# Layer 1's four wide chunks as a split group, its subtraction on VectorE

## The chip, the cores and the metric

The kernel runs on one core of a Trainium2 chip. The metric is the time of one execution on the device, in microseconds (us), and the time shown is the median of several runs. A separate execution, recorded by the hardware profiler, gives the profile and the trace.

## The reference

A "compressed interaction network" of three layers over x0 of shape 512 x 32 x 64 (batch, field, depth). Each layer multiplies every row of its input h with every row of x0, mixes the products with a weight matrix, adds a bias and applies ReLU:

```
for i in range(3):
    Wk = Ws[i].reshape(128, H, 32)              # H = 32 in layer 1, 64 in layers 2 and 3
    xk = relu(einsum('bhd,bmd,ohm->bod', h, x0, Wk) + b[i])
    if i != 2:  outs.append(xk[:, :64]); h = xk[:, 64:]
    else:       outs.append(xk)
y = concatenate([o.sum(axis=-1) for o in outs], axis=1)     # 512 x 256
```

All arithmetic is in float32.

## The kernel before, in words

The 512 x 64 (batch, depth) pairs are 32768 columns, in 64 tiles of T = 512 columns. Products of rows h and m of one tile are laid out as chunks of 128 partitions: layer 1 needs 5 chunks (the symmetric pairs are folded by adding two weight arrangements), layers 2 and 3 need 16 each, taken as four groups (q = 0 to 3) of G = 4 chunks. A chunk is one matmul of a 128x128 weight with a 128x512 product.

A float32 matmul takes two passes of TensorE. A group can be *split* instead: ScalarE rounds the product ZS to a type that TensorE multiplies in one pass (`high`, ZH), GpSimd or VectorE subtracts to get the rest (`low`, ZL = ZS - ZH), and the weights are split in the same way at the start. Three sets of four fast matmuls (WL x ZH, WH x ZH, WH x ZL) then stand in for four float32 ones. Groups 0, 1 and 3 of layers 2 and 3 are split; group 2 is *plain* (float32, through the wide buffer ZW), and so is all of layer 1 (four chunks through ZW, the fifth through the narrow buffer ZN).

All orders are written out by hand, with one instruction stream for each engine and semaphores between them. Iteration i works on layer 1 of tile i, layer 2 of tile i-1 and layer 3 of tile i-2.

- VectorE (L252 to L278) makes the products: layer 1 and ZN (L199), four of layer 2, the sum of layers 1 and 2 (L237), four of layer 3, with one subtraction (L228, that of layer 2's group 3) after layer 3's first product, then the sum of layer 3 (L242). Layer 1's product reads XDP, which is the copy in PSUM of XD; the others read HP, the copy in PSUM of H. All read X from SBUF.
- ScalarE (L340 to L363) does the rounding (L313), the copies of XD (L300) and of H (L306), and the ReLUs (L324, L329, L332). The copy of XD for tile i+1 stands between the rounding of layer 2's group 3 and that of layer 3's group 0.
- GpSimd (L280 to L292) does five subtractions a tile (L291).
- TensorE (L410 to L434): layer 1, layer 2, layer 3, in that order.
- SyncE (L160 to L172) issues all DMAs, on one queue, in this order in iteration i: XD of tile i+1 (four pieces of 64 KB, L139), X of tile i+1 (four pieces of 512 KB, L134), the spread of H of tile i after layer 1's ReLU, the spread of H of tile i-1 after layer 2's ReLU (L145, L148: five pieces inside SBUF).

ZS, ZH and ZL have three slots each. A product waits until the subtraction three groups back is done; a rounding and a subtraction wait until TensorE has finished the group three back. ZW has two slots, XD two, X four.

Of the kernel before, what the change touches and what calls it, by code (L numbers as in the profile page):

```python
# [6 lines left out]
HID, OUT = 64, 128  # L7
# [8 lines left out]
G = 4  # L16
Q = 4
PLAIN = 2
SPLIT = (0, 1, 3)
BY_DVE = ((1, 2),)  # L20
NS = len(SPLIT)
# [15 lines left out]
def wide_before(i, layer):  # L37

    n = sum(live(k - l) for k in range(i) for l in range(3))
    return n + sum(live(i - l) for l in range(layer))  # L40


def split_before(i, layer, k):

    n = NS * sum(live(s - l) for s in range(i) for l in (1, 2))
    return n + NS * sum(live(i - l) for l in range(1, layer)) + k


def lows_before(n, by_dve):

    order = [(layer, k) for i in range(TILES + 2) for layer in (1, 2) if live(i - layer) for k in range(NS)]
    return sum((u in BY_DVE) == by_dve for u in order[:n])


def cin_kernel(nc, xpad, w1, w1t, w2, w3, bias, ident_in, out):
# [4 lines left out]
    with ctx:  # L60
# [9 lines left out]
        W1 = sb("W1", [128, C1, OUT])  # L70
        WF = sb("WF", [128, 2, G, OUT])
# [6 lines left out]
        XD = sb("XD", [128, 2, T])  # L78
# [12 lines left out]
        WS = ZS[:, 0:2, 0:NS, :].rearrange("p w n (g o) -> p w n g o", g=G)  # L91
        OUTS = XD[:, :, :].rearrange("p a (b c) -> p (a b) c", b=2)
# [10 lines left out]
        w1_summed, w_high, w_low = sem("w1_summed"), sem("w_high"), sem("w_low")  # L103
        cleared = sem("cleared")
        x_loaded = [sem(f"x_loaded{n}") for n in range(XSLOTS)]
        xd_loaded = [sem(f"xd_loaded{n}") for n in range(2)]
# [14 lines left out]
        def wait_lows(engine, n):  # L121

            if lows_before(n, False):
                engine.wait_ge(low_by_pool, lows_before(n, False))
            if lows_before(n, True):
                engine.wait_ge(low_by_dve, lows_before(n, True))

        @block.sync
        def _(sp):
            def load_x(t):  # L130
                slot = t % XSLOTS
                for k in range(NB):
                    src = bass.AP(xpad.tensor, k * TOK + t * T, [[TOK, BLK], [NB * TOK, XC], [1, T]])
                    sp.dma_start(X[BLK * k:BLK * k + BLK, slot, :, :], src).then_inc(x_loaded[slot], 16)  # L134

            def load_xd(t):
                for k in range(NB):
                    src = bass.AP(xpad.tensor, t * T, [[TOK, BLK], [1, T]])
                    sp.dma_start(XD[BLK * k:BLK * k + BLK, t % 2, :], src).then_inc(xd_loaded[t % 2], 16)  # L139
# [12 lines left out]
            load_xd(0)  # L152
            load_x(0)
            sp.dma_start(bias_sb[:, :], bias).then_inc(small_loaded, 16)
            sp.dma_start(ident[:, :], ident_in).then_inc(small_loaded, 16)
            for w, wd in enumerate((w2, w3)):
                for n, q in enumerate(SPLIT):
                    sp.dma_start(WS[:, w, n, :, :], wd[:, G * q:G * q + G, :]).then_inc(ws_loaded[w], 16)  # L158
                sp.dma_start(WF[:, w, :, :], wd[:, G * PLAIN:G * PLAIN + G, :]).then_inc(wf_loaded[w], 16)
            for i in range(TILES + 2):  # L160
                t = i + 1
                if live(t):
                    if t >= 2:
                        sp.wait_ge(xd_copied, t - 1)
                    load_xd(t)
                    if t >= XSLOTS:
                        sp.wait_ge(prod_ready, split_before(t - XSLOTS + 2, 2, NS - 1) + 1)
                    load_x(t)
                if live(i):
                    spread_hidden(i, 0)  # L170
                if live(i - 1):
                    spread_hidden(i - 1, 1)  # L172
            for n in range(BLOCKS):
                sp.wait_ge(outs_ready, n + 1)
                sp.dma_start(out[128 * n:128 * n + 128, :], OUTS[:, n, :]).then_inc(stored, 16)
            sp.wait_ge(stored, 16 * BLOCKS)

        @block.vector
        def _(dve):
# [7 lines left out]
            dve.wait_ge(w1_summed, 4)  # L187

            def wide_slot(i, layer):
                n = wide_before(i, layer)  # L190
# [8 lines left out]
            def layer1(i):  # L199
                x = X[:, i % XSLOTS, :, :]  # L200
                to = wide_slot(i, 0)
                dve.wait_ge(xd_copied, i + 1)
                dve.wait_ge(x_loaded[i % XSLOTS], 16 * NB * (i // XSLOTS + 1))
                nc.vector.tensor_tensor(to, over(XDP[:, :], G), x[:, 0:G, :], ALU.mult).then_inc(wide_ready, 1)  # L204
                if i >= 1:
                    dve.wait_ge(narrow_used, i)
                nc.vector.tensor_tensor(ZN[:, :], XDP[:, :], x[:, G, :], ALU.mult).then_inc(narrow_ready, 1)

            def product(i, layer, q):
# [42 lines left out]
            for i in range(TILES + 3):  # L252
# [15 lines left out]
                if live(i - 1):  # L268
                    low(i, 1, 2)
# [11 lines left out]
        def _(pool):  # L281
            for i in range(TILES + 2):
                for layer in (1, 2):
                    for k in range(NS) if live(i - layer) else ():
                        if (layer, k) in BY_DVE:
                            continue
                        n = split_before(i, layer, k)
                        if n >= SSLOTS:
                            pool.wait_ge(split_used, n - SSLOTS + 1)
                        pool.wait_ge(high_ready, n + 1)  # L290
                        nc.gpsimd.tensor_tensor(ZL[:, n % SSLOTS, :, :], ZS[:, n % SSLOTS, :, :],  # L291
                                                ZH[:, n % SSLOTS, :, :], ALU.subtract).then_inc(low_by_pool, 1)  # L292

        @block.scalar
        def _(act):
            def copy_xd(t):
                act.wait_ge(xd_loaded[t % 2], 16 * NB * (t // 2 + 1))
                if t >= 1:
                    act.wait_ge(narrow_ready, t)
                nc.scalar.activation(XDP[:, :], XD[:, t % 2, :], ACT.Copy).then_inc(xd_copied, 1)  # L300

            def copy_hidden(t, layer):
                act.wait_ge(h_loaded[layer], 16 * (1 + NB) * (t + 1))
                if t >= 1:
# [29 lines left out]

            for w in range(2):
# [30 lines left out]
        def _(pe):  # L366
            def layer1(i):
                if i == 0:
                    pe.wait_ge(w1_summed, 4)
                else:  # L370
                    pe.wait_ge(relu_done[0], i)
                n = wide_before(i, 0)
                pe.wait_ge(wide_ready, n + 1)
# [6 lines left out]
            def plain(i, layer):  # L380
                n = wide_before(i, layer)
# [6 lines left out]
            def split(i, layer, q):  # L388
                k = SPLIT.index(q)
                n = split_before(i, layer, k)  # L390
# [7 lines left out]
                wait_lows(pe, n + 1)  # L398
# [11 lines left out]
            for i in range(TILES + 2):  # L410
                if live(i):
                    layer1(i)
                for layer in (1, 2):
# [7 lines left out]
                    for q in range(Q):  # L421
# [7 lines left out]
                        if q == PLAIN:  # L429
                            plain(i, layer)  # L430
# [38 lines left out]
```

## Time and profile before

| | |
|---|---|
| median of 3 runs | 1852.87 us (1852.87 to 1853.91) |
| profiled execution, its own time | 1851.87 us |
| its span | 1850.1 us |
| busy: TensorE, VectorE, GpSimd, ScalarE | 1799.3, 1552.2, 1468.3, 1095.6 us |
| DMA queue of SyncE | 204.68 MB, 52.5% of 16 engines' span |
| X, to landing, median of 256 pieces | 9.0 us |
| XD, to landing, median of 256 pieces | 2.0 us |

The busy time of an engine counts its instructions. A matmul's length in the trace is modelled and overlaps the next, so for TensorE the distance from one start to the next is what a matmul costs. VectorE's and ScalarE's instructions overlap their successors a little too. A bracket at the end of a timeline row gives the idle time of the engine before the instruction and what ended it.

### The profile page before, as it was taken

The numbers are of one execution on the slowest core, as the hardware profiler recorded it, in microseconds if no ns is written. First come the engines' busy times: TensorE is split into PE (matmuls) and PEld (weight loads), VectorE is DVE, ScalarE is ACT, GpSimd is POOL, SyncE is SP. The second block draws the span as 40 slices with busy tenths as digits, with TensorE's granted clock in tenths as the row PEclk, the third lists the DMA queues.
The fourth block names the chain that finished last, engine by engine and source line by source line (L and its number), as shares of the span: only waits on it lengthen the run. The fifth ranks groups of instructions, "written<-read, shape, count | busy, mean of one in ns | idle before, by whom it ended". The sixth has DMA issues, their size and how long they took to land.

```text
span 1850.1 us, 18063 instructions
## 1 busy us (share of the span) xinstructions
PE 1799.3 (97%) x6284; PEld 1184.3 (64%) x6284; DVE 1552.2 (84%) x853; ACT 1095.6 (59%) x899; POOL 1468.3 (79%) x324
## 2 busy tenths in 40 slices
PE   3899999999999999999999999999999999999997
PEld 1566666666666666666666666666666666666665
DVE  3998898898898888888888888888888888988974
ACT  2566656656656666566565665665666666566562
POOL 0788878878878778778778778778778788788786
PEclk9999999999999999999999999999999999999998
DMA  8565455465465564564564564564564554654610
GB/s 201 111 123 121 98 122 116 101 125 114 100 128 107 105 128 105 106 129 103 107 129 102 109 128 99 114 128 93 121 128 92 122 125 92 125 122 95 126 26 20
DMA packets 119513, 205.83 MB, mean 111 GB/s; under 512 B 18816, under 2 KB 19968, under 8 KB 119424
## 3 DMA queue, kind: packets, MB, share of 16 engines
q1 hardware_dynamic: 119424, 204.68, 52.5%
q8 instruction: 51, 0.84, 0.2%
q14 instruction: 38, 0.31, 0.1%
HBM read 153.75 MB, written 0.52 MB: 83 GB/s over the span
## 4 chain that ended last, share of the span: by engine, by line
PE 96%; POOL 1%; DMA 1%; SPq 1%; ACT 1%; DVE 0%; issue 0%; DVEq 0%; POOLq 0%; ACTq 0%
PE ACC L384 24%; PE ACC L400 19%; PE ACC L394 19%; PE ACC L397 19%; PE ACC L375 12%; PE ACC L378 3%; POOL ZL L291 1%; DMA ZS<-in_w 1%; ACT ZH L313 0%; DVE ZS L221 0%; SPq L158 0%; DVE ZW L204 0%; ACT HP L306 0%; DMA H<-H 0%; SPq L139 0%
## 5 line engine op out<-in xcount | busy, mean ns | idle before, releaser
L291 POOL TENSOR_TENSOR ZL<-ZS,ZH 128x2048 fp32r<-128x2048 f32 x320 | 1468.1, 4617 | 372.8 <-ACT ZH L313 372.8
L313 ACT ACTIVATE ZH<-ZS 128x2048 fp32r<-128x2048 f32 x384 | 734.2, 1912 | 536.7 <-PE ACC L400 415.0
L221 DVE TENSOR_TENSOR ZS<-HP,X 128x2048 f32<-128x2048 f32 x384 | 870.5, 2281 | 150.9 <-ACT HP L306 149.6
L394 PE MATMUL ACC<-ZH,WL 128*128 128x512 f32 x1536 | 497.5, 446 | 7.3 <-ACT ZH L313 7.3
L384 PE MATMUL ACC<-ZW,WF 128*128 128x512 f32 x1024 | 460.2, 592 | 0.0
L400 PE MATMUL ACC<-ZL,WH 128*128 128x512 f32 x1536 | 421.7, 396 | 8.4 <-POOL ZL L291 8.3
L397 PE MATMUL ACC<-ZH,WH 128*128 128x512 f32 x1536 | 421.0, 396 | 0.0
L394 PEld LDWEIGHTS ACC<-ZH,WL 128*128 128x128 f32 x1536 | 289.9, 189 | 151.7 <-issue 98.9
L216 DVE TENSOR_TENSOR ZW<-HP,X 128x2048 f32<-128x2048 f32 x128 | 292.2, 2283 | 101.3 <-PE ACC L384 101.3
L400 PEld LDWEIGHTS ACC<-ZL,WH 128*128 128x128 f32 x1536 | 287.9, 188 | 81.6 <-POOL ZL L291 11.7
L397 PEld LDWEIGHTS ACC<-ZH,WH 128*128 128x128 f32 x1536 | 288.8, 188 | 70.2
L384 PEld LDWEIGHTS ACC<-ZW,WF 128*128 128x128 f32 x1024 | 194.0, 189 | 195.1 <-issue 183.7
L375 PE MATMUL ACC<-ZW,W 128*128 128x512 f32 x512 | 233.6, 599 | 30.8 <-DVE ZW L204 30.8
L375 PEld LDWEIGHTS ACC<-ZW,W 128*128 128x128 f32 x512 | 98.2, 192 | 131.1 <-issue 125.5
L204 DVE TENSOR_TENSOR ZW<-XDP,X 128x2048 f32<-128x2048 f32 x64 | 145.6, 2275 | 22.0 <-ACT XDP L300 18.0
L228 DVE TENSOR_TENSOR ZL<-ZS,ZH 128x2048 fp32r<-128x2048 f32 x64 | 157.7, 2464 | 1.4 <-ACT ZH L313 1.4
L324 ACT ACTIVATE R<-ACC,bias_sb 128x512 f32<-128x512 f32 x64 | 44.0, 688 | 170.4 <-PE ACC L400 170.4
L306 ACT ACTIVATE HP<-H 128x1024 f32<-128x1024 f32 x128 | 129.9, 1015 | 9.8 <-DMA H<-H 9.8
L329 ACT ACTIVATE H<-ACC,bias_sb 64x512 f32<-64x512 f32 x128 | 86.6, 676 | 9.4 <-PE ACC L378 5.1
L332 ACT ACTIVATE R<-ACC,bias_sb 64x512 f32<-64x512 f32 x128 | 87.5, 684 | 1.6
L378 PE MATMUL ACC<-ZN,W 128*128 128x512 f32 x128 | 65.4, 592 | 0.0
L237 DVE TENSOR_REDUCE S<-R 128x8 f32<-128x512 f32 (+1 forms) x65 | 43.9, 675 | 2.7 <-ACT R L332 2.7
(32 smaller groups left out, 165.0 us busy)
## 6 DMA issues: line engine op xcount, KB each, us to landing
X<-in_xpad SPq DMA_DIRECT2D x256, 512.0 KB, 9.0
H<-H SPq DMA_DIRECT2D x512, 64.0 KB, 2.0
XD<-in_xpad SPq DMA_DIRECT2D x256, 64.0 KB, 2.0
H<-H SPq DMA_DIRECT2D x128, 128.0 KB, 2.2
ZS<-in_w SPq DMA_DIRECT2D x6, 256.0 KB, 11.4
WF<-in_w SPq DMA_DIRECT2D x2, 256.0 KB, 11.9
out<-XD SPq DMA_DIRECT2D x4, 128.0 KB, 1.8
W<-in_w SPq DMA_DIRECT2D x1, 320.0 KB, 3.0
```

Source lines behind the costliest of these rows:

```text
L204: nc.vector.tensor_tensor(to, over(XDP[:, :], G), x[:, 0:G, :], ALU.mult).then_inc(wide_ready, 1)
L216: nc.vector.tensor_tensor(wide_slot(i, layer), h, x, ALU.mult).then_inc(wide_ready, 1)
L221: nc.vector.tensor_tensor(ZS[:, n % SSLOTS, :, :], h, x, ALU.mult).then_inc(prod_ready, 1)
L228: nc.vector.tensor_tensor(ZL[:, n % SSLOTS, :, :], ZS[:, n % SSLOTS, :, :], ZH[:, n % SSLOTS, :, :], ALU.subtract).then_inc(low_by_dve, 1)
L291: nc.gpsimd.tensor_tensor(ZL[:, n % SSLOTS, :, :], ZS[:, n % SSLOTS, :, :], ZH[:, n % SSLOTS, :, :], ALU.subtract).then_inc(low_by_pool, 1)
L306: nc.scalar.activation(HP[layer][:, :, :], H[layer][:, :, :], ACT.Copy).then_inc(h_copied[layer], 1)
L313: nc.scalar.activation(ZH[:, n % SSLOTS, :, :], ZS[:, n % SSLOTS, :, :], ACT.Copy).then_inc(high_ready, 1)
L375: last = nc.tensor.matmul(ACC[0][:, :], W1[:, g, :], ZW[:, n % WSLOTS, g, :], start=(g == 0), stop=False)
L384: last = nc.tensor.matmul(ACC[layer][:, :], WF[:, layer - 1, g, :], ZW[:, n % WSLOTS, g, :], start=False, stop=False)
L394: nc.tensor.matmul(ACC[layer][:, :], wl[:, g, :], ZH[:, n % SSLOTS, g, :], start=(k == 0 and g == 0), stop=False)
L397: nc.tensor.matmul(ACC[layer][:, :], wh[:, g, :], ZH[:, n % SSLOTS, g, :], start=False, stop=False)
L400: last = nc.tensor.matmul(ACC[layer][:, :], wh[:, g, :], ZL[:, n % SSLOTS, g, :], start=False, stop=(k == NS - 1 and g == G - 1))
```

## The change

The group description becomes a table: which groups of each layer are split, which are plain, and which engine subtracts. Layer 1's four wide chunks are a split group now. There are seven split groups a tile in place of six, and two plain ones through ZW in place of three. VectorE subtracts for layer 1 and for group 3 of layer 2, GpSimd for the other five. The weights W1 are split at the start into W1H (ScalarE) and W1L (VectorE). The copy of XD of tile 0 comes before the rounding of W2 and W3. XD has one buffer in place of two, loaded after X instead of before it, and the stages for W2 and W3 lie in X slots 2 and 3. A product waits only for the engine that did the subtraction three groups back. The numbers `SPLIT_NO` and `PLAIN_NO` count the groups in the order in which they are worked on.

```
+SPLIT = {0: (0,), 1: (0, 1, 3), 2: (0, 1, 3)}
+PLAIN = {0: (), 1: (2,), 2: (2,)}
+LOW_BY = {
+    (0, 0): "dve",
+    (1, 0): "pool", (1, 1): "pool", (1, 3): "dve",
+    (2, 0): "pool", (2, 1): "pool", (2, 3): "pool",
+}
...
+        W1H, W1L = sb("W1H", [128, G, OUT], f32r), sb("W1L", [128, G, OUT], f32r)
-        XD = sb("XD", [128, 2, T])
+        XD = sb("XD", [128, T])
-        WS = ZS[:, 0:2, 0:NS, :].rearrange("p w n (g o) -> p w n g o", g=G)
+        WS = X[:, 2:4, 0:NS, :].rearrange("p w n (g o) -> p w n g o", g=G)
...
@@ SyncE, iteration i, t = i + 1
-                    if t >= 2:
-                        sp.wait_ge(xd_copied, t - 1)
+                    if t == 2:
+                        sp.wait_ge(w_low, 2)
+                    if t >= XSLOTS:
+                        sp.wait_ge(prod_ready, SPLIT_NO[t - XSLOTS + 2, 2, Q - 1] + 1)
+                    load_x(t)
+                    sp.wait_ge(xd_copied, t)
                     load_xd(t)
-                    if t >= XSLOTS:
-                        sp.wait_ge(prod_ready, split_before(t - XSLOTS + 2, 2, NS - 1) + 1)
-                    load_x(t)
...
@@ VectorE
-            dve.wait_ge(w1_summed, 4)
+            dve.wait_ge(w1_high, 1)
+            nc.vector.tensor_tensor(W1L[:, :, :], W1[:, 0:G, :], W1H[:, :, :], ALU.subtract).then_inc(w1_low, 1)
...
                 x = X[:, i % XSLOTS, :, :]
-                to = wide_slot(i, 0)
+                n = SPLIT_NO[i, 0, 0]
+                if n >= SSLOTS:
+                    wait_low(dve, n - SSLOTS)
                 dve.wait_ge(xd_copied, i + 1)
...
-                nc.vector.tensor_tensor(to, over(XDP[:, :], G), x[:, 0:G, :], ALU.mult).then_inc(wide_ready, 1)
+                nc.vector.tensor_tensor(ZS[:, n % SSLOTS, :, :], over(XDP[:, :], G), x[:, 0:G, :],
+                                        ALU.mult).then_inc(prod_ready, 1)
...
                 if live(i - 1):
-                    for q in range(Q):
+                    product(i, 1, 0)
+                if live(i):
+                    low(i, 0, 0)
+                if live(i - 1):
+                    for q in range(1, Q):
                         product(i, 1, q)
...
                 if live(i - 1):
-                    low(i, 1, 2)
+                    low(i, 1, 3)
...
@@ ScalarE
+            act.wait_ge(w1_summed, 4)
+            nc.scalar.activation(W1H[:, :, :], W1[:, 0:G, :], ACT.Copy).then_inc(w1_high, 1)
+            copy_xd(0)
...
             act.wait_ge(small_loaded, 32)
-            copy_xd(0)
             for i in range(TILES + 2):
+                if live(i):
+                    high(i, 0, 0)
                 if live(i - 1):
                     high(i, 1, 0)
...
@@ TensorE, layer1(i)
                 for g in range(G):
-                    last = nc.tensor.matmul(ACC[0][:, :], W1[:, g, :], ZW[:, n % WSLOTS, g, :], start=(g == 0), stop=False)
-                last.then_inc(wide_used, 1)
+                    nc.tensor.matmul(ACC[0][:, :], W1L[:, g, :], ZH[:, n % SSLOTS, g, :], start=(g == 0), stop=False)
+                for g in range(G):
+                    nc.tensor.matmul(ACC[0][:, :], W1H[:, g, :], ZH[:, n % SSLOTS, g, :], start=False, stop=False)
                 pe.wait_ge(narrow_ready, i + 1)
-                nc.tensor.matmul(ACC[0][:, :], W1[:, G, :], ZN[:, :], start=False, stop=True).then_inc(narrow_used, 1)
+                nc.tensor.matmul(ACC[0][:, :], W1[:, G, :], ZN[:, :], start=False, stop=False).then_inc(narrow_used, 1)
+                wait_low(pe, n)
+                for g in range(G):
+                    last = nc.tensor.matmul(ACC[0][:, :], W1H[:, g, :], ZL[:, n % SSLOTS, g, :],
+                                            start=False, stop=(g == G - 1))
+                last.then_inc(split_used, 1)
```

ScalarE's ReLU of layer 1 waits for this last group instead of for the narrow chunk.

## Rows read from the trace of the kernel before

**Rows 1.** The page: busy line and chain; then waits: us in total, times, longest.

```profile
PE 1799.3 (97%) x6284; PEld 1184.3 (64%) x6284; DVE 1552.2 (84%) x853; ACT 1095.6 (59%) x899; POOL 1468.3 (79%) x324
PE 96%; POOL 1%; DMA 1%; SPq 1%; ACT 1%; DVE 0%; issue 0%; DVEq 0%; POOLq 0%; ACTq 0%
...
PE ACC L400 <- POOL ZL L291: 8.3, 5, 2.5
```

**Rows 2.** TensorE timeline, start and length in us: first matmul, then two tiles.

```profile
26.78 5.33 PE L375 MATMUL ACC<-ZW,W 128*128 128x512 f32 x8 [26.78 <-DVE ZW L204]
...
875.21 3.60 PE L375 MATMUL ACC<-ZW,W 128*128 128x512 f32 x8
...
903.16 3.60 PE L375 MATMUL ACC<-ZW,W 128*128 128x512 f32 x8
906.59 1.02 PE L378 MATMUL ACC<-ZN,W 128*128 128x512 f32 x2
...
910.24 1.09 PE L394 MATMUL ACC<-ZH,WL 128*128 128x512 f32 x4
...
913.04 3.60 PE L384 MATMUL ACC<-ZW,WF 128*128 128x512 f32 x8
```

**Rows 3.** GpSimd timeline of one tile, idle time before in brackets.

```profile
898.83 9.12 POOL L291 TENSOR_TENSOR ZL<-ZS,ZH 128x2048 fp32r<-128x2048 f32 x2 [0.52 <-ACT ZH L313]
912.50 13.76 POOL L291 TENSOR_TENSOR ZL<-ZS,ZH 128x2048 fp32r<-128x2048 f32 x3 [4.55 <-ACT ZH L313]
```

**Rows 4.** VectorE timeline of the same tile.

```profile
904.96 0.68 DVE L237 TENSOR_REDUCE S<-R 128x8 f32<-128x512 f32 x1
905.56 2.28 DVE L221 TENSOR_TENSOR ZS<-HP,X 128x2048 f32<-128x2048 f32 x1
907.75 2.34 DVE L228 TENSOR_TENSOR ZL<-ZS,ZH 128x2048 fp32r<-128x2048 f32 x1
910.02 2.28 DVE L221 TENSOR_TENSOR ZS<-HP,X 128x2048 f32<-128x2048 f32 x1
```

**Rows 5.** ScalarE timeline of the same tile.

```profile
906.96 0.58 ACT L300 ACTIVATE XDP<-XD 128x512 f32<-128x512 f32 x1
...
919.47 1.92 ACT L313 ACTIVATE ZH<-ZS 128x2048 fp32r<-128x2048 f32 x1 [3.91 <-PE ACC L400]
921.29 1.01 ACT L306 ACTIVATE HP<-H 128x1024 f32<-128x1024 f32 x1
922.24 0.67 ACT L329 ACTIVATE H<-ACC,bias_sb 64x512 f32<-64x512 f32 x1
922.92 0.69 ACT L332 ACTIVATE R<-ACC,bias_sb 64x512 f32<-64x512 f32 x1
```

**Rows 6.** Early timeline of GpSimd and VectorE.

```profile
44.33 9.12 POOL L291 TENSOR_TENSOR ZL<-ZS,ZH 128x2048 fp32r<-128x2048 f32 x2 [43.88 <-ACT ZH L313]
...
50.88 4.72 DVE L228 TENSOR_TENSOR ZL<-ZS,ZH 128x2048 fp32r<-128x2048 f32 x1 [1.40 <-ACT ZH L313]
...
71.31 4.40 DVE L228 TENSOR_TENSOR ZL<-ZS,ZH 128x2048 fp32r<-128x2048 f32 x1
...
64.42 15.74 POOL L291 TENSOR_TENSOR ZL<-ZS,ZH 128x2048 fp32r<-128x2048 f32 x3 [10.97 <-ACT ZH L313]
```

**Rows 7.** SyncE queue: issues, start and length in us.

```profile
923.63 0.50 SPq L145 DMA_DIRECT2D H<-H  x1
926.71 2.40 SPq L139 DMA_DIRECT2D XD<-in_xpad  x4
929.15 1.90 SPq L134 DMA_DIRECT2D X<-in_xpad  x4
```

**Rows 8.** Landings: XD of 11.7 to 13.2; H of 75.38; X of 929.15 to 930.6.

```profile
DMA to landing us min/median/max: 10.9/11.0/11.7
...
DMA to landing us min/median/max: 5.5/5.5/5.5
...
DMA to landing us min/median/max: 5.5/8.6/11.3
```

More of the change, by code:

```diff
@@ L17 @@
 Q = 4
[L18 to L21, printed above, removed]
+SPLIT = {0: (0,), 1: (0, 1, 3), 2: (0, 1, 3)}
[5 more added lines that the diff above has]
+}
+NS = 3
 XSLOTS, WSLOTS, SSLOTS = 4, 2, 3
@@ L34, in live, with in_order @@
     return 0 <= t < TILES
[L37 to L52, printed above, removed]
+def in_order(which):
+    return {g: n for n, g in enumerate(
+        (i, layer, q) for i in range(TILES + 2) for layer in range(3) if live(i - layer) for q in which[layer])}
+SPLIT_NO, PLAIN_NO = in_order(SPLIT), in_order(PLAIN)
+LOW_OF = [LOW_BY[layer, q] for _, layer, q in SPLIT_NO]
+LOW_COUNT = [LOW_OF[:n + 1].count(LOW_OF[n]) for n in range(len(LOW_OF))]
 def cin_kernel(nc, xpad, w1, w1t, w2, w3, bias, ident_in, out):
@@ L102, in cin_kernel @@
         small_loaded = sem("small_loaded")
-        w1_summed, w_high, w_low = sem("w1_summed"), sem("w_high"), sem("w_low")
+        w1_summed, w1_high, w1_low = sem("w1_summed"), sem("w1_high"), sem("w1_low")
+        w_high, w_low = sem("w_high"), sem("w_low")
         cleared = sem("cleared")
         x_loaded = [sem(f"x_loaded{n}") for n in range(XSLOTS)]
-        xd_loaded = [sem(f"xd_loaded{n}") for n in range(2)]
+        xd_loaded = sem("xd_loaded")
         xd_copied = sem("xd_copied")
@@ L119, in cin_kernel, with wait_low @@
         block = ctx.enter_context(nc.Block())
[L121 to L126, printed above, removed]
+        def wait_low(engine, n):
+            if LOW_OF[n] == "pool":
+                engine.wait_ge(low_by_pool, LOW_COUNT[n])
+            else:
+                engine.wait_ge(low_by_dve, LOW_COUNT[n])
         @block.sync
@@ L156, in _ @@
             for w, wd in enumerate((w2, w3)):
-                for n, q in enumerate(SPLIT):
+                for n, q in enumerate(SPLIT[1 + w]):
                     sp.dma_start(WS[:, w, n, :, :], wd[:, G * q:G * q + G, :]).then_inc(ws_loaded[w], 16)
-                sp.dma_start(WF[:, w, :, :], wd[:, G * PLAIN:G * PLAIN + G, :]).then_inc(wf_loaded[w], 16)
+                sp.dma_start(WF[:, w, :, :], wd[:, G * PLAIN[1 + w][0]:G * PLAIN[1 + w][0] + G, :]).then_inc(wf_loaded[w], 16)
             for i in range(TILES + 2):
@@ L186, in _, with wide_slot @@
             nc.vector.memset(S12[0:HID, B:B + BT], 0.0).then_inc(cleared, 1)
-            dve.wait_ge(w1_summed, 4)
-            def wide_slot(i, layer):
-                n = wide_before(i, layer)
+            dve.wait_ge(w1_high, 1)
+            nc.vector.tensor_tensor(W1L[:, :, :], W1[:, 0:G, :], W1H[:, :, :], ALU.subtract).then_inc(w1_low, 1)
+            def wide_slot(i, layer, q):
+                n = PLAIN_NO[i, layer, q]
                 if n >= WSLOTS:
@@ L282, in _ @@
             for i in range(TILES + 2):
[L283 to L292, printed above, removed]
+                for layer in range(3):
+                    for q in SPLIT[layer] if live(i - layer) else ():
+                        if LOW_BY[layer, q] == "pool":
+                            n = SPLIT_NO[i, layer, q]
+                            if n >= SSLOTS:
+                                pool.wait_ge(split_used, n - SSLOTS + 1)
+                            pool.wait_ge(high_ready, n + 1)
+                            nc.gpsimd.tensor_tensor(ZL[:, n % SSLOTS, :, :], ZS[:, n % SSLOTS, :, :],
+                                                    ZH[:, n % SSLOTS, :, :], ALU.subtract).then_inc(low_by_pool, 1)
         @block.scalar
@@ L296, in copy_xd @@
             def copy_xd(t):
-                act.wait_ge(xd_loaded[t % 2], 16 * NB * (t // 2 + 1))
+                act.wait_ge(xd_loaded, 16 * NB * (t + 1))
                 if t >= 1:
                     act.wait_ge(narrow_ready, t)
-                nc.scalar.activation(XDP[:, :], XD[:, t % 2, :], ACT.Copy).then_inc(xd_copied, 1)
+                nc.scalar.activation(XDP[:, :], XD[:, :], ACT.Copy).then_inc(xd_copied, 1)
             def copy_hidden(t, layer):
@@ L304, in copy_hidden @@
                 if t >= 1:
-                    act.wait_ge(prod_ready, split_before(t + layer, layer + 1, NS - 1) + 1)
+                    act.wait_ge(prod_ready, SPLIT_NO[t + layer, layer + 1, Q - 1] + 1)
                 nc.scalar.activation(HP[layer][:, :, :], H[layer][:, :, :], ACT.Copy).then_inc(h_copied[layer], 1)
             def high(i, layer, q):
-                n = split_before(i, layer, SPLIT.index(q))
+                n = SPLIT_NO[i, layer, q]
                 if n >= SSLOTS:
@@ L316, in relu @@
                 if layer == 0:
-                    act.wait_ge(narrow_used, t + 1)
+                    act.wait_ge(split_used, SPLIT_NO[t, 0, 0] + 1)
                 else:
-                    act.wait_ge(split_used, split_before(t + layer, layer, NS - 1) + 1)
+                    act.wait_ge(split_used, SPLIT_NO[t + layer, layer, Q - 1] + 1)
                 b = bias_sb[:, layer:layer + 1]
@@ L388, in split @@
             def split(i, layer, q):
-                k = SPLIT.index(q)
-                n = split_before(i, layer, k)
+                k = SPLIT[layer].index(q)
+                n = SPLIT_NO[i, layer, q]
                 wh, wl = WH[:, layer - 1, k, :, :], WL[:, layer - 1, k, :, :]
@@ L397, in split @@
                     nc.tensor.matmul(ACC[layer][:, :], wh[:, g, :], ZH[:, n % SSLOTS, g, :], start=False, stop=False)
[L398 removed]
+                wait_low(pe, n)
                 for g in range(G):
@@ L428, in _ @@
                                 turn(n)
-                        if q == PLAIN:
-                            plain(i, layer)
+                        if q in PLAIN[layer]:
+                            plain(i, layer, q)
                         else:
```

26 lines of the change are left out of this document (13 added, 13 removed).

## The prediction

> **What bounds the kernel now.** I read the page's busy line and chain first, then the waits, then one tile in the timelines. TensorE is busy 97% and holds 96% of the chain; no other engine ends more than 1% of it [rows 1]. In 1850 us the matmuls waited for GpSimd 8.3 us in all, 5 times [rows 1]. So each tile costs what its matmuls cost. Layer 1's matmuls start at 875.21 and again at 903.16 [rows 2]: a tile is 27.95 us. In it a float32 group of four chunks (eight passes) runs from 903.16 to the narrow chunk's start at 906.59: 3.43 us, 0.428 a pass, and the narrow chunk has two passes more. A split group of twelve passes runs from 910.24 to 913.04: 2.80 us, 0.233 a pass [rows 2]. Sum: 26 x 0.428 (layer 1's ten passes, sixteen of the two plain groups) + 6 x 2.80 = 27.9 us. The others fit inside. GpSimd does five subtractions, 3 in 13.76 us and 2 in 9.12, and idles 4.55 us before the three [rows 3].
>
> **TensorE's part.** Layer 1's eight float32 passes become twelve fast ones: 3.43 becomes 2.80 us, the narrow chunk's 0.86 stays. TensorE then needs 7 x 2.80 + 0.86 + 2 x 3.43 = 27.3 us a tile: -0.63 us, at most -40 us over 64 tiles. That is the gain if everything else keeps up.
>
> **The others' work.** ScalarE gets one more rounding, 1.91 us [rows 5], on about 17.1 us a tile: it has room for work, not necessarily for a wait. GpSimd keeps five subtractions (22.9 us). VectorE: nine products at 2.20 us from start to start, three short ones (ZN and two sums) at 0.60, and now two subtractions at 2.27 (907.75 to 910.02) [rows 4]: 19.8 + 1.8 + 4.54 = 26.1 us, 1.2 below TensorE's 27.3. The product of layer 1 is the same work in another buffer. The plain products no longer wait for a wide slot (two a tile for two slots); that wait was slack. The waits for one subtraction only, in place of both counts, can only come earlier; I take nothing.
>
> **The subtraction on VectorE excludes GpSimd's.** Two stretches show it [rows 6]. VectorE's subtraction, 2.34 us alone, took 4.72 us from 50.88 while GpSimd's pair ran until 53.45; it ended 2.15 us after that pair. The one at 71.31 took 4.40: GpSimd's second of three had ended at about 73.5, VectorE finished 2.2 us later, and GpSimd's three took 15.74 us in place of 13.76. So whichever asks second waits for the whole instruction of the other, then takes 2.16 (VectorE) or 4.45 us (GpSimd). In the steady tile VectorE's one subtraction falls at 907.75 to 910.09, just into GpSimd's idle time (907.95 to 912.50) [rows 3, 4]. Two no longer do so for free: 22.9 + 2 x 2.16 = 27.2 us of one shared path. The Trainium skill (GPSIMD Engine Reference, 1. Specifications) says that GpSimd shares its SBUF interfaces with VectorE, with contention when a VectorE instruction has two SBUF inputs; it has no price, the trace agrees and prices it. The products read PSUM and X and show no such stretch. Without that rule the sum is rival B's.
>
> Where they fall follows from the slots. Call a tile's split groups a (layer 1), b, c, d (layer 2), e, f, g (layer 3), with L for the subtraction. VectorE's order is a, ZN, b, La, c, plain, d, sum, e, Ld, f, plain, g, sum; GpSimd's is Lb, Lc, Le, Lf, Lg. A product waits for the subtraction three groups back, so b waits for the Lf of the tile before and c for its Lg. La is asked for 2.2 us into Lg and waits for its end. The loop Ld, Le, Lf, Lg, La, c, plain, d, sum, e, Ld is then 4.45 + 9.16 + 2.16 - 0.08 + 9.40 + 2.35 = 27.45 us. Alone this would make the tile 27.45 in place of 27.95.
>
> **The moved XD transfer.** XD has one buffer now and SyncE issues X(i+1) before XD(i+1). Of X four issues go ahead (2.1 MB), then four of XD (0.26 MB). Before, XD(i+1) was issued first, at 926.71 to 929.11 in one tile [rows 7], and took 2.0 us to landing (the table's median), so it was there at 931.1, 4 us before its copy (906.96 in the tile before, so 934.9 here) [rows 5]. X's first issue, 929.15, is 5.5 us after the start of layer 2's spread at 923.63; without XD in front it comes where XD's was, 926.71, 3.08 us after it [rows 7]. X's four, issued 929.15 to 930.6, land 5.5, then up to 11.3 us after their own issue: the last is there 12.7 us after the first issue [rows 7, 8]. XD has to pass this data. That it queues is seen at the start: XD issued at 11.68, behind 2 MB of weights, lands after 10.9 to 11.7 us, and a spread piece issued at 75.38 behind X takes 5.5 in place of 2.0 [rows 8]. An eighth of X's data at X's pace (2.1 MB in about 10.7 us) is 1.3 us, so all of XD is there 13.9 us after X's first issue. Bounds: below 12.0 (the spread piece landed about 0.6 us ahead of X's last), above 14.5. The Trainium skill (DMA: Bandwidth & Descriptors, Queues, rings and completion order) has descriptors of one queue consumed in ring order, with no barrier between their writes; it too speaks for XD behind X, and by it the landing could be a little ahead of X's, which is my lower bound.
>
> ScalarE copies XD(i+1) in tile i between the rounding of d and the rounding of e. It is in order, so e, f, g's rounding, layer 1's ReLU and all subtractions behind them stand behind this copy. The XD of a tile can be asked for only once ReLU 2 (ScalarE's last work of the tile before) is done. One tile round that way is 3.1 + 13.9 + copy and rest of ScalarE's tile (10.0) = 27.0 us with no wait in it, but there are waits in it, and the longest way round takes two tiles. From XD landed:
> - copy 0.55 and rounding of e 1.91 [rows 5]: 2.46; hand-over to GpSimd 0.14
> - Le, Lf, Lg 13.76 [rows 3]: 16.36
> - La 2.16, less 0.08 of overlap: 18.44
> - c, plain, d, sum, e: 3 x 2.20 + 0.60 + 2.20 = 9.40: 27.84
> - Ld 2.27, f and plain 4.40, g 2.28, hand-over 0.10: 36.89
> - rounding of g, copy of H2, ReLU 2 (two): 1.82 + 0.95 + 0.70 + 0.69 = 4.16 [rows 5]: 41.05
> - spread issued 3.10 [rows 7]: 44.15; X and XD 13.9: 58.05.
> Half is 29.03 us a tile. I checked the other waits against this: rounding of g (asked for at 7.7 after XD, done 9.6) is ready before Lf ends at 11.8; H2's spread lands at about 9.0, its copy is at 9.5; Lc ends at 27.55, before Ld is asked for at 27.84; TensorE's 27.3 fits. All hold, so 29.03 repeats.
>
> **Sum.** 29.03 - 27.95 = 1.08 us; 63 tiles copy a next XD: +68 us. The start: X(1) and XD(1) swap, layer 1's ReLU of tile 0 stands behind XD(1), about 2 us; W1's rounding and subtraction are new; the rows nearest to them are a copy and a sum over the same 128x512 size, 0.58 us on ScalarE [rows 5] and 0.68 for a short instruction of VectorE [rows 4]. They lie before X(0) has landed, the first matmul being at 26.8 [rows 2], so I cost them at nothing; with that cover gone they are 1.3 us, once. W2's staging in X slots 2 and 3 holds X(2) until w_low, about 31 us, and SyncE is at that point later anyway. Taken: +2. The profiled execution's own time is 1851.87 (span 1850.1), 1.00 below the median 1852.87: 1851.87 + 70 = 1922 us, 1923 against the median. I give 1922.
>
> **Rivals.**
> A. XD is not late: it lands less than 11.7 us after X's first issue (the point where (44.15 + L)/2 reaches 27.95), below 10.8 the loop of 27.45 decides. For: the pieces of a transfer land separately. Against: [rows 8]. Time: 1851.87 - 63 x 0.50 + 2 = 1822 us.
> B. The two engines' subtractions run side by side in the steady state. La then costs nothing behind Lg: (58.05 - 2.08)/2 = 27.98, so 1852 + 2 + 2 = 1856, no gain and hardly a loss. Against: the same two stretches [rows 6].
> C. The hand-over goes worse: Ld is asked for just after GpSimd took Lc (margin here 0.3 us) and waits another 2.2 to 4.5 us. (58.05 + 4.5)/2 = 31.3 every tile is 2060, (58.05 + 2.2)/2 = 30.1 is 1990, and once in a few tiles 1950. For: the margin is thin. Against: Lc, if late, makes Ld wait only for its rest.
>
> **How the numbers follow.** Forecast 0.72, A 0.13, B 0.06, C 0.09. The forecast's own range is L from 12.0 to 14.5, tile 28.1 to 29.3: 1862 to 1941. To leave out no more than 2 in 10 I take in B and the lower part of C: 1855 to 1955; A and the rest of C stay outside. About 0.2% (3.7 us) is what a measurement can tell. Faster: A and a little of B, 0.14. Within: most of B, 0.05. Slower: the rest, 0.81.
>
> **What would show it.** Right: ScalarE's XDP copy waits for XD's landing in nearly every tile, about 2 us (d's rounding ends at 27.1, XD at 29.0), some 120 us; XD's issue to landing goes from 2.0 to about 12 us; VectorE's layer 1 subtraction lasts about 4.4 us and layer 2's 2.35; TensorE's busy time falls by 40 us while it waits 1.7 us a tile for a subtraction of GpSimd. Wrong: XD landing in under 10 us, or TensorE still without gaps, or both subtractions of VectorE at 2.35 us.

## The result: 1925 us, 3.9% slower than before

The changed kernel takes 1924.99 us (median of 4 runs, 1924.16 to 1926.34) beside 1852.87 for the kernel before: ratio 1.039, interval 1.0377 to 1.0403. The prediction was 1922 us, slower with 0.81, range 1855 to 1955.

The page of the changed kernel, span, busy line, chain by engine and by line; the rows of before that answer to the middle two are [rows 1]:

```profile
span 1923.2 us, 18198 instructions
PE 1797.3 (93%) x6540; PEld 1224.5 (64%) x6540; DVE 1798.7 (94%) x918; ACT 1221.4 (64%) x964; POOL 1591.7 (83%) x324
DVE 29%; issue 19%; DMA 17%; POOL 14%; SPq 11%; ACT 7%; PE 2%; ACTq 0%; DVEq 0%; POOLq 0%
DMA XD<-in_xpad 17%; POOL ZL L298 14%; DVE ZL L232 11%; DVE ZS L225 10%; DVE ZW L220 7%; SPq L147 4%; ACT ZH L320 4%; SPq L133 4%; SPq L138 2%; ACT HP L313 2%; ACT R L339 1%; DVE S L241 1%; ACT H L336 1%; SPq L144 1%; PE ACC L401 1%
```

TensorE went from 96% of the chain to 2%. In its place stands a ring of all the others: XD's landing, GpSimd's and VectorE's subtractions, VectorE's products, SyncE's issues, ScalarE. It is still busy 93%: busy does not say what bounds. (The letters a to g for a tile's split groups and La to Lg for their subtractions are those of the prediction.)

The waits of the changed kernel (us in total, times, longest):

```profile
ACT XDP L307 <- DMA XD<-in_xpad: 128.1, 62, 8.8
...
PE ACC L417 <- POOL ZL L298: 71.2, 70, 2.1
```

The copy of XD waits for its landing in nearly every tile, 2 us each; before it waited for a landing not once. TensorE waits for a GpSimd subtraction 70 times in place of 5 [rows 1].

One tile of the changed kernel: GpSimd, then VectorE's b, La and c, then its e, Ld and f, then ScalarE's copy of XD, then SyncE. They answer to [rows 3], [rows 4], [rows 5] and [rows 7]:

```profile
924.80 25.02 POOL L298 TENSOR_TENSOR ZL<-ZS,ZH 128x2048 fp32r<-128x2048 f32 x5 [3.85 <-ACT ZH L320]
```

```profile
934.14 2.29 DVE L225 TENSOR_TENSOR ZS<-HP,X 128x2048 f32<-128x2048 f32 x1 [0.71 <-POOL ZL L298]
936.35 4.37 DVE L232 TENSOR_TENSOR ZL<-ZS,ZH 128x2048 fp32r<-128x2048 f32 x1
940.63 2.28 DVE L225 TENSOR_TENSOR ZS<-HP,X 128x2048 f32<-128x2048 f32 x1
...
947.82 2.27 DVE L225 TENSOR_TENSOR ZS<-HP,X 128x2048 f32<-128x2048 f32 x1
950.02 2.28 DVE L232 TENSOR_TENSOR ZL<-ZS,ZH 128x2048 fp32r<-128x2048 f32 x1
952.22 2.28 DVE L225 TENSOR_TENSOR ZS<-HP,X 128x2048 f32<-128x2048 f32 x1
```

```profile
922.23 0.60 ACT L307 ACTIVATE XDP<-XD 128x512 f32<-128x512 f32 x1 [1.76 <-DMA XD<-in_xpad]
...
951.90 0.60 ACT L307 ACTIVATE XDP<-XD 128x512 f32<-128x512 f32 x1 [2.58 <-DMA XD<-in_xpad]
```

```profile
934.29 0.50 SPq L144 DMA_DIRECT2D H<-H  x1
934.83 2.71 SPq L147 DMA_DIRECT2D H<-H  x4
937.59 2.08 SPq L133 DMA_DIRECT2D X<-in_xpad  x4
939.72 1.84 SPq L138 DMA_DIRECT2D XD<-in_xpad  x4
```

X's first issue is at 937.59 and XD is landed at 951.9: 14.3 us; in the tile before, 908.69 and 922.2, 13.5. Over the 47 copies between 300 and 1650 us the mean from X's first issue to the copy is 13.95 us, the least 12.1 and the most 14.8. GpSimd starts its row at 924.80, 2.6 us after the copy's start, and works 25.02 us without a gap: five subtractions, 22.9, and VectorE's La of 2.16 in the middle. La took 4.37 us, Ld 2.28.

How long a tile is can be read over the whole middle: copies of XD between 300 and 1650 us, their count, then first and last start. Changed kernel:

```profile
L307 ACT ACTIVATE XDP<-XD x47: 601/602/605, 312.8 to 1647.3; 128x512 f32<-128x512 f32 x47
```

(1647.3 - 312.8) / 46 = 29.01 us. The kernel before has 48 copies from 320.1 to 1633.6, 27.95. The same is done for each experiment below. Single tiles of the changed kernel last from 28.05 to 30.20 us, those of the kernel before from 27.66 to 28.24. Two tiles together last from 57.48 to 58.75: a long tile is mostly followed by a short one, as it should be if one way of two tiles sets the pace.

The chain shows this way itself. Here it is from one landing of XD to the next one in it, with the pieces between the main ones left out:

```profile
883.40 9.97 DMA XD<-in_xpad
...
895.96 3.13 POOL ZL L298
...
907.62 4.24 DVE ZL L232
...
921.17 2.28 DVE ZL L232
...
930.14 0.04 ACT ZH L320
...
933.58 0.69 ACT R L339
...
937.59 0.57 SPq L133
...
941.14 10.74 DMA XD<-in_xpad
```

XD is landed at 893.37 and again at 951.88. The landing of the tile between them (the copy at 922.23) is not in the chain. From the first landing it is 2.59 us to Le, 18.49 to the end of La, 27.80 to Ld, 36.77 to the rounding of g, 40.90 to the end of ReLU 2, 44.22 to X's first issue and 58.51 to the next landing; the prediction has 2.60, 18.44, 27.84, 36.89, 41.05, 44.15 and 58.05. Between 300 and 1650 us there are 47 copies of XD, and its landing stands 24 times in the chain. The first two are 28.5 us apart; all others are 57.5 to 58.8 apart, 58.04 in the mean. One thing the chain cannot show: that La stands behind Lg. That wait has no semaphore, so its 2 us count as VectorE's.

### The profile page after: what moved, and what is told of

Its sections match the earlier page's. It is cut to its first block, busy times and chain, and to the rows that moved or that the text cites. A ratio compares the mean times of both kernels' runs of the same rounds, so it can differ in the third digit from the quotient of the medians.

```text
span 1923.2 us, 18198 instructions
## 1 busy us (share of the span) xinstructions
PE 1797.3 (93%) x6540; PEld 1224.5 (64%) x6540; DVE 1798.7 (94%) x918; ACT 1221.4 (64%) x964; POOL 1591.7 (83%) x324
## 4 chain that ended last, share of the span: by engine, by line
DVE 29%; issue 19%; DMA 17%; POOL 14%; SPq 11%; ACT 7%; PE 2%; ACTq 0%; DVEq 0%; POOLq 0%
DMA XD<-in_xpad 17%; POOL ZL L298 14%; DVE ZL L232 11%; DVE ZS L225 10%; DVE ZW L220 7%; SPq L147 4%; ACT ZH L320 4%; SPq L133 4%; SPq L138 2%; ACT HP L313 2%; ACT R L339 1%; DVE S L241 1%; ACT H L336 1%; SPq L144 1%; PE ACC L401 1%
## 5 line engine op out<-in xcount | busy, mean ns | idle before, releaser
L298 POOL TENSOR_TENSOR ZL<-ZS,ZH 128x2048 fp32r<-128x2048 f32 x320 | 1591.5, 5002 | 322.1 <-ACT ZH L320 320.6
L320 ACT ACTIVATE ZH<-ZS 128x2048 fp32r<-128x2048 f32 x448 | 855.3, 1912 | 516.2 <-DVE ZS L225 514.2
L417 PE MATMUL ACC<-ZL,WH 128*128 128x512 f32 x1536 | 435.7, 405 | 73.9 <-POOL ZL L298 71.2
L411 PE MATMUL ACC<-ZH,WL 128*128 128x512 f32 x1536 | 473.7, 430 | 6.1 <-ACT ZH L320 6.1
L232 DVE TENSOR_TENSOR ZL<-ZS,ZH 128x2048 fp32r<-128x2048 f32 x128 | 412.1, 3219 | 15.0 <-ACT ZH L320 14.8
L207 DVE TENSOR_TENSOR ZS<-XDP,X 128x2048 f32<-128x2048 f32 x64 | 145.7, 2277 | 16.6 <-DMA X<-in_xpad 9.4
L307 ACT ACTIVATE XDP<-XD 128x512 f32<-128x512 f32 x64 | 38.5, 601 | 128.1 <-DMA XD<-in_xpad 128.1
L386 PE MATMUL ACC<-ZH,W1L 128*128 128x512 f32 x256 | 72.6, 406 | 41.6 <-ACT ZH L320 41.6
L393 PE MATMUL ACC<-ZL,W1H 128*128 128x512 f32 x256 | 95.9, 496 | 0.0
L386 PEld LDWEIGHTS ACC<-ZH,W1L 128*128 128x128 f32 x256 | 48.9, 192 | 54.1 <-issue 42.4
L388 PE MATMUL ACC<-ZH,W1H 128*128 128x512 f32 x256 | 72.5, 406 | 0.0
## 6 DMA issues: line engine op xcount, KB each, us to landing
XD<-in_xpad SPq DMA_DIRECT2D x256, 64.0 KB, 10.4
```

The lines of the kernel that those rows point to most:

```text
L207: nc.vector.tensor_tensor(ZS[:, n % SSLOTS, :, :], over(XDP[:, :], G), x[:, 0:G, :], ALU.mult).then_inc(prod_ready, 1)
L232: nc.vector.tensor_tensor(ZL[:, n % SSLOTS, :, :], ZS[:, n % SSLOTS, :, :], ZH[:, n % SSLOTS, :, :], ALU.subtract).then_inc(low_by_dve, 1)
L320: nc.scalar.activation(ZH[:, n % SSLOTS, :, :], ZS[:, n % SSLOTS, :, :], ACT.Copy).then_inc(high_ready, 1)
L386: nc.tensor.matmul(ACC[0][:, :], W1L[:, g, :], ZH[:, n % SSLOTS, g, :], start=(g == 0), stop=False)
L411: nc.tensor.matmul(ACC[layer][:, :], wl[:, g, :], ZH[:, n % SSLOTS, g, :], start=(k == 0 and g == 0), stop=False)
L417: last = nc.tensor.matmul(ACC[layer][:, :], wh[:, g, :], ZL[:, n % SSLOTS, g, :], start=False, stop=(k == NS - 1 and g == G - 1))
```

## The experiments

The theory is that of the prediction: a way round through the XD transfer and the two engines' exclusive subtractions, which takes two tiles. The rivals are that one of the two is enough, that XD's landing is paid in every tile, or that VectorE's load is the bound. Ratios are to the kernel before on the same chip; its median beside them was 1852.2 to 1852.6.

### XD first

```
+                    sp.wait_ge(xd_copied, t)
+                    load_xd(t)
                     if t == 2:
                         sp.wait_ge(w_low, 2)
...
                     load_x(t)
-                    sp.wait_ge(xd_copied, t)
-                    load_xd(t)
```

> The changed kernel with XD of tile i+1 issued before X of tile i+1 again, still with one XD buffer. Theory (XD queues behind X's 2.1 MB, and this wait is one link of a way round that takes two tiles): XD lands about 2 us after its issue, ScalarE's copy no longer waits, and the loop through the two engines' subtractions, 27.45 us a tile, decides: 1825 us. Rival 1 (the mutual exclusion of the subtractions or VectorE's load alone makes the tile 29 us): 1915 to 1925 us. Rival 2 (XD alone, nothing else near the bound): 27.3 us a tile, 1814 us.

1824.2 us, ratio 0.985 (0.983 to 0.986), 27.45 us a tile. So the order of two issues on SyncE turns the change from +3.9% to -1.5%. VectorE and GpSimd of this run:

```profile
925.08 2.28 DVE L232 TENSOR_TENSOR ZL<-ZS,ZH 128x2048 fp32r<-128x2048 f32 x1
...
940.22 2.98 DVE L232 TENSOR_TENSOR ZL<-ZS,ZH 128x2048 fp32r<-128x2048 f32 x1 [0.68 <-ACT ZH L320]
...
952.51 2.27 DVE L232 TENSOR_TENSOR ZL<-ZS,ZH 128x2048 fp32r<-128x2048 f32 x1
```

```profile
927.31 13.75 POOL L298 TENSOR_TENSOR ZL<-ZS,ZH 128x2048 fp32r<-128x2048 f32 x3 [2.43 <-ACT ZH L320]
942.06 10.24 POOL L298 TENSOR_TENSOR ZL<-ZS,ZH 128x2048 fp32r<-128x2048 f32 x2 [1.00 <-ACT ZH L320]
954.74 9.22 POOL L298 TENSOR_TENSOR ZL<-ZS,ZH 128x2048 fp32r<-128x2048 f32 x2 [2.44 <-ACT ZH L320]
```

The loop is there link by link: Ld ends at 927.36, GpSimd's three end at 941.06, La ends 2.14 us behind them at 943.20, the next Ld at 954.78, and 954.74 - 927.31 = 27.43 us after its start GpSimd's row of three begins again.

### VectorE's subtractions without a second SBUF operand

```
+                zh = ZH[:, n % SSLOTS, :, :]
+                if 2 <= i < TILES:
+                    zh = over(HP[0 if layer == 0 else 1][:, 0, :], G)
-                nc.vector.tensor_tensor(ZL[...], ZS[...], ZH[:, n % SSLOTS, :, :], ALU.subtract)
+                nc.vector.tensor_tensor(ZL[...], ZS[...], zh, ALU.subtract)
```

> The changed kernel, XD still behind X, but VectorE's two subtractions read ZS and a tile in PSUM in place of ZS and ZH, so they have one SBUF operand only; the values subtracted are not the ones needed. Theory: layer 1's subtraction lasts 2.2 us in place of 4.3, GpSimd's five no longer stretch, and the two-tile way loses 2.0 us, one a tile: 28.0 us, 1860 us. Rival (XD alone sets the tile): 1925 us as before it. Rival (the exclusion alone): 27.3 us, 1814 us.

1867.6 us, ratio 1.008 (1.0063 to 1.0097), 28.11 us a tile, 0.9 less than the changed kernel. VectorE, b, La and c of this run:

```profile
909.50 2.29 DVE L225 TENSOR_TENSOR ZS<-HP,X 128x2048 f32<-128x2048 f32 x1 [1.77 <-POOL ZL L301]
911.71 2.28 DVE L235 TENSOR_TENSOR ZL<-ZS,HP 128x2048 fp32r<-128x2048 f32 x1
913.97 2.29 DVE L225 TENSOR_TENSOR ZS<-HP,X 128x2048 f32<-128x2048 f32 x1
```

La is 2.28 us, and GpSimd's mean is 4.63 in place of 5.00. The instruction's size, engine and place are the same. Its second operand lies in PSUM and not in SBUF (and is one row of 512 values read four times, like that of the products), so the stretch is contention between the two engines for SBUF operands. What this run computes is not the sum needed. The Trainium skill (GPSIMD Engine Reference, 1. Specifications) names this contention; the runs agree, and add its price. The tile is 0.1 us longer than the 28.0 expected, 8 us in all; a way that probably explains it is found below. This run is also rival B made true: the two subtractions no longer stand in each other's way. Its 1856 us was 12 us too low.

### Both edits

The edits are those of the last two sections together.

> Both edits together: XD before X, and VectorE's two subtractions with one SBUF operand (the values subtracted are not the ones needed). Theory: nothing is left but TensorE's 27.3 us a tile: 1814 us. If VectorE's work of 26.1 us with its waits were the bound by itself, it would stay above 1840.

1814.2 us, ratio 0.979 (0.978 to 0.981), 27.32 us a tile, with TensorE 95% of the chain again. That is what the split alone would give.

### The kernel before, with XD behind X

```
-                    if t >= 2:
-                        sp.wait_ge(xd_copied, t - 1)
-                    load_xd(t)
                     if t >= XSLOTS:
                         sp.wait_ge(prod_ready, split_before(t - XSLOTS + 2, 2, NS - 1) + 1)
                     load_x(t)
+                    if t >= 2:
+                        sp.wait_ge(xd_copied, t - 1)
+                    load_xd(t)
```

> The kernel before, with only the order of its SyncE issues changed: X of tile i+1 first, then XD of tile i+1 (two XD buffers as before). Theory: XD lands about 12 us after its issue, but the two-tile way has neither layer 1's subtraction nor its exclusion and is about 26.7 us a tile, under TensorE's 27.95: no change, 1853 to 1858 us. Rival (a late XD by itself costs about 1 us a tile in either kernel): 1915 us or more.

Missed: 1889.3 us, ratio 1.020 (1.018 to 1.021), 28.46 us a tile. Neither the theory's "no change" nor the rival's 1915. Its chain and one tile of GpSimd and TensorE:

```profile
PE 40%; POOL 17%; DMA 16%; issue 9%; SPq 6%; DVE 6%; ACT 5%; ACTq 0%; POOLq 0%; DVEq 0%
```

```profile
907.63 22.85 POOL L291 TENSOR_TENSOR ZL<-ZS,ZH 128x2048 fp32r<-128x2048 f32 x5 [6.22 <-ACT ZH L313]
```

```profile
916.90 1.19 PE L400 MATMUL ACC<-ZL,WH 128*128 128x512 f32 x4 [0.85 <-POOL ZL L291]
917.92 3.60 PE L384 MATMUL ACC<-ZW,WF 128*128 128x512 f32 x8
```

TensorE waits for the second of GpSimd's row (Lf), which ends at about 916.8, and from there has no gap to the end of layer 2's last group at about 940.4. There is a second two-tile way, which I had not counted. From XD landed:

- copy and rounding of e, Le and Lf: 11.75 us
- the last matmuls of f: 1.0
- plain, g, layer 1, b, c, plain, d on TensorE (layer 1 in float32): 22.3
- ScalarE: 4.2; SyncE's issues of the spread: 3.1
- X and XD: 14.3 and 14.7 in the tiles read.

That is about 56.8, 28.4 a tile. My expectation had TensorE go on from e, not from f. The sum was made after the result, and its last term is taken from the tiles read: with the mean of all 48 copies, 14.0, it is 28.2 a tile, and 0.25 us of the 28.46 stay open. In the changed kernel this way is 0.6 us shorter, since layer 1 is, about 28.1 a tile with the longer landing and 27.9 with the mean. That is near the tile of the run with subtractions of one SBUF operand (28.11, TensorE 32% of its chain), and below the 29.0 of the first way.

### XD behind three pieces of X

```
-                    load_x(t)
+                    load_x(t, 0, NB - 1)
                     sp.wait_ge(xd_copied, t)
                     load_xd(t)
+                    load_x(t, NB - 1, NB)
```

> The changed kernel with XD issued behind three of X's four pieces, the fourth behind XD. XD should land about 11.9 us after X's first issue in place of 14.0. Theory (XD's landing is paid once in two tiles): the tile falls by half of 2.1 us, from 29.0 to 28.0, 1859 us; the way through TensorE, which the run with only the order of issues changed in the kernel before brought to light, is 0.1 us below that. Rival (XD's landing is paid in every tile, ScalarE's own round): it falls by the whole 2.1 us until the 27.45 of the subtractions' loop decides, 1825 us.

1858.7 us, ratio 1.0034 (1.0022 to 1.0046), 28.00 us a tile. As expected, the tile did not fall to 27.45, so XD's landing is not paid in every tile. From SyncE and ScalarE of one tile of this run the landing is read again:

```profile
906.13 1.59 SPq L133 DMA_DIRECT2D X<-in_xpad  x3
907.77 1.85 SPq L138 DMA_DIRECT2D XD<-in_xpad  x4
```

```profile
917.65 0.60 ACT L308 ACTIVATE XDP<-XD 128x512 f32<-128x512 f32 x1 [1.16 <-DMA XD<-in_xpad]
```

11.5 us from X's first issue to the copy, 2 to 2.8 less than with four pieces ahead, and the tile lost 1.01, about a half. By itself this run is the weaker witness for the two tiles: XD's landing has 5% of its chain and stands there 7 times for 49 copies, in place of 17% and 24 times for 47. Part of that is the wait that the chain cannot show; how much was not worked out.

### The copy of XD two roundings later

```
-                if live(i + 1):
-                    copy_xd(i + 1)
                 if live(i - 2):
                     high(i, 2, 0)
...
                     high(i, 2, 1)
+                if live(i + 1):
+                    copy_xd(i + 1)
+                if live(i - 2):
                     high(i, 2, 3)
```

> The changed kernel, XD still behind all of X, but ScalarE copies XD only between the roundings of layer 3's groups 1 and 3, two roundings and a ReLU later. Theory: what costs is that the rounding of layer 3's group 0, and GpSimd's row of three behind it, stand behind the wait in ScalarE's order; now XD is there before it is asked for, and the loop of 27.45 us decides: 1825 us. Rival (the late XD costs wherever it is copied, through VectorE's layer 1 product): 1900 us or more.

1825.7 us, ratio 0.985 (0.984 to 0.987), 27.46 us a tile, with XD as late as ever (10.4 us from issue to landing). The copy waits once, 1.7 us in all. So a late transfer costs nothing by itself; what costs is the row of work behind the instruction that waits for it.

### The plain product ahead of the subtraction

This comes on top of the edit that puts XD first. The lines `if live(...)` are left out here:

```
 product(i, 1, 0)
+product(i, 1, 2)
 low(i, 0, 0)
-for q in range(1, Q):
+for q in (1, 3):
     product(i, 1, q)
```

> The changed kernel with XD before X, and VectorE's plain product of layer 2 moved ahead of its layer 1 subtraction, into the time in which GpSimd works on the last of its three. Theory: the loop of the subtractions loses the 2.2 us of that product (27.45 to 25.25), VectorE no longer stands waiting, and TensorE's 27.3 us decides: 1815 us. Rival (VectorE's own work of 26.1 us and its waits for ScalarE decide in the run with XD first): 1824 us, unchanged against that run.

Missed: 1852.9 us, ratio 1.0002 (0.9992 to 1.0011), 27.83 us a tile, 29 us slower than with XD first alone. VectorE's La, e and Ld, and GpSimd:

```profile
905.39 2.27 DVE L232 TENSOR_TENSOR ZL<-ZS,ZH 128x2048 fp32r<-128x2048 f32 x1
...
913.54 2.29 DVE L225 TENSOR_TENSOR ZS<-HP,X 128x2048 f32<-128x2048 f32 x1 [0.89 <-ACT HP L315]
915.75 3.17 DVE L232 TENSOR_TENSOR ZL<-ZS,ZH 128x2048 fp32r<-128x2048 f32 x1
```

```profile
905.79 10.97 POOL L300 TENSOR_TENSOR ZL<-ZS,ZH 128x2048 fp32r<-128x2048 f32 x2 [1.09 <-ACT ZH L322]
917.98 14.54 POOL L300 TENSOR_TENSOR ZL<-ZS,ZH 128x2048 fp32r<-128x2048 f32 x3 [1.22 <-ACT ZH L322]
```

La now comes 0.7 us after GpSimd's three end (at 904.7) instead of at their end: with the plain product there, VectorE's own work from Ld to La is 14.3 us (918.92 to 933.21) and has no gap in it, while GpSimd's three take 13.6 from Ld's end. GpSimd's pair is behind it, Ld behind the pair (3.17 us). What I left out is that the loop has two sides between La and Ld: VectorE's c to e, 9.4 us, and GpSimd's Lb and Lc, 9.1. Shortening the first by 2.2 could bring 0.3 at most, and the later La costs 0.7: 27.45 - 0.3 + 0.7 = 27.85. La, the pair behind it, Ld behind the pair and VectorE's work up to the next La give the same: 2.2 + 9.2 + 2.2 + 14.3 = 27.9. This was worked out after the result, from one tile.

The same edit in the changed kernel, with XD still behind X:

> The changed kernel with XD still behind X, and only the plain product of layer 2 moved ahead of VectorE's layer 1 subtraction. Theory: the two-tile way loses 2.2 us, so the tile falls by 1.1 to 27.9, but the way through TensorE holds it at 28.2 as in the run with subtractions of one SBUF operand: 1867 us. Rival (VectorE's stalls are hidden behind the XD wait): 1925 us.

Missed for the same reason: 1925.1 us, ratio 1.039 (1.037 to 1.041), 28.92 us a tile, 0.1 below the changed kernel. The rival had the number, but not by its reason: VectorE's stall at La is gone, and it comes back at Ld (3.14 us in one tile) and at e (0.9 us idle), behind GpSimd's pair and ScalarE's copy of H for layer 3. From the end of Lg, La, Lb and Lc, then Ld behind them take 2.20 + 9.16 + 2.16 = 13.52 us, where La, VectorE's five and Ld are 13.75 by the prediction: 0.2 us in two tiles.

### Two tests of the way through TensorE

The first is the kernel before with XD behind three pieces of X, by the same edit as above. Both expectations have 28.65 us a tile for XD behind all of X; read from the copies it is 28.46.

> The kernel before with XD issued behind three of X's four pieces. With XD behind all four it was 28.65 us a tile. Theory (two-tile way, through TensorE: XD landed, roundings, GpSimd's first two of the row, then layer 3's last groups, layer 1 and layer 2 on TensorE, layer 2's ReLU, the spread, X, XD): an earlier landing by 2.1 us takes 1.05 off, 27.6, under TensorE's own 27.95, so the time is that of the kernel before, 1852 to 1855 us. Rival (XD's landing counts little there and something else makes the 28.65): 1870 us or more.

1857.0 us, ratio 1.0025 (1.0015 to 1.0034): 27.95 us a tile, TensorE 95% of the chain. As expected in the tiles; the 4.4 us over the kernel before lie outside the middle, and I did not trace them.

The second leaves out one of layer 1's chunks, and has X issued before XD as well (that edit is shown above):

```
-                for g in range(G):
+                for g in (0, 1, 3):
                     last = nc.tensor.matmul(ACC[0][:, :], W1[:, g, :], ...)
```

> The kernel before with XD behind all of X (28.65 us a tile), and one of layer 1's four wide chunks left out of the matmuls (its result is not the sum needed): TensorE has 0.86 us less a tile, two passes. Theory: TensorE's work from layer 3's group 1 to layer 2's last group is a link of the two-tile way, so the tile falls by half of 0.86, to 28.2: 1862 us. Rivals: TensorE is not in that way: 1889 us, unchanged; TensorE is the bound in every tile: 1834 us.

1867.8 us, ratio 1.0084 (1.0069 to 1.0099). The copies of XD, first with all four chunks, then with three:

```profile
L300 ACT ACTIVATE XDP<-XD x48: 601/602/604, 307.8 to 1645.2; 128x512 f32<-128x512 f32 x48
```

```profile
L300 ACT ACTIVATE XDP<-XD x48: 601/602/603, 306.4 to 1625.0; 128x512 f32<-128x512 f32 x48
```

28.46 and 28.06 us a tile: 0.40 less for 0.86 less of TensorE's work, a half, as a link of a two-tile way should be (0.43). Both rivals are out: unchanged, and less by the whole 0.86. Not excluded is a third, that another way of about 28.06 took over before the 0.86 were used up; TensorE has 7% of this run's chain, against 40% with all four chunks. The run is 6 us slower than expected in the median, and I did not follow where.

## Why the prediction was right

1. *TensorE would no longer bound.* Right: 2% of the chain. With both obstacles gone the tile is 27.32 us, against 27.3 worked out for seven split groups.
2. *XD queues behind X, 13.9 us from X's first issue to all of XD.* Right: 13.5 and 14.3 in the two tiles read, 13.95 in the mean. "About 12 us" holds from XD's own first issue to its copy (11.4 and 12.2 in these tiles); the profile's median of 10.4 is that of single pieces, the last of which is issued 1.4 us after the first.
3. *VectorE's and GpSimd's subtractions exclude each other, La pays and Ld does not.* Right: 4.37 and 2.28 us against 4.4 and 2.35. Shown by moving the second operand to PSUM, where La takes 2.28.
4. *The loop through the subtractions is 27.45 us.* Right: 27.45 in the run with XD first, and 27.46 with the copy moved. That it fits to the hundredth is luck: the terms as written add up to 27.44, and Ld, put at 2.35, takes 2.28. Rival A's 1822 us was in truth the price of this loop alone; it measures 1824 once its condition is made true.
5. *A two-tile way of 58.05 us, 29.03 a tile.* 29.01 measured. That it takes two tiles is shown by the chain, where XD's landing comes back every 58.04 us, with the sum right within 0.15 us up to X's first issue in the stretch followed; XD behind three pieces fits (-1.01 for about -2.1). That it needs both links is shown by the runs that take one out (27.45 and 28.11). The last link, the landing, varies from 12.1 to 14.8 us, so that 29.01 meets 29.03 so closely is in part luck.
6. *"TensorE's 27.3 fits."* True, but it looks at TensorE's own work only: there is a second two-tile way through TensorE, about 28 us a tile in this kernel. Nothing in the forecast hung on it, being below 29.0. It decided two of the experiments.
7. *Start, +2.* The first product of layer 2 begins at 41.71 in place of 40.01: +1.7. 1.06 us in 63 tiles is 67; with the start that leaves about 3 us of the 72, some of it at the end, where the time from the spread issued just ahead of the last X to the last instruction is 118.3 in place of 116.0.
8. *TensorE's busy time falls by 40 us.* Wrong as a sign: it is 1797.3 in place of 1799.3, since the modelled lengths of its matmuls grow around waits. In the run with XD first, with 5.5 us of such waits in place of 71.2, it is 1767.7, still 8 us short of the 40. The wait for GpSimd is 71.2 us in all, 1.1 a tile, where 1.7 were forecast; the rest of the 1.7 is probably inside those lengths.

Rival B fell with [rows 6] confirmed. Its price was also too low, 1856 us where the run that makes its condition true takes 1867.6, because it left out the way through TensorE. Rival C did not come: in the middle of the changed kernel every Ld takes 2.27 or 2.28 us. In the tile of the chain above Lc ends at 920.96 and Ld begins at 921.17, so the margin was 0.2 us.

## What to carry to other kernels

Before moving a DMA on its queue, add what lies ahead of it there to its landing, and then look at which in-order engine waits for it and what stands behind that wait: here one swap of issues, or one copy moved two places down, is worth 100 us. When several engines hand work round, write down the closed ways with their lengths and the number of tiles that each takes, both sides of every fork; an engine at 93% busy may be in none that sets the pace. The changed kernel with XD issued first, 1824 us, beats both kernels.

## What the runs showed of the hardware

That the two engines exclude each other was read from the trace before the prediction; the runs make it firm. VectorE and GpSimd subtractions that each read two SBUF operands do not slow each other by degrees: whichever comes second stands until the other instruction is over, so a 2.3 us instruction lasts up to 4.7 us, and GpSimd's 2.0 us longer than its 4.6 [rows 6]. In the changed kernel that makes GpSimd's mean 5.00 us a subtraction. With VectorE's second operand in PSUM its time is 2.28 us, whatever GpSimd does, and GpSimd's mean is 4.63.

What I had not expected is how much the landing of a small transfer behind a large one varies: the copy of XD begins from 12.1 to 14.8 us after the first issue of the large one, in a kernel whose tiles otherwise repeat to a few hundredths (27.42 to 27.58 us with XD first).
